# x of the first two batches loaded in halves, and one low part of the last adapter made earlier

## The reference

```python
w = L0_cond_weight[itok_B_1_14]                  # (8, 512, 512), gathered
y = jnp.einsum('bij,bkj->bik', x, w)             # x is (8, 128, 512)
q = y[:, 107:-1, :].mean(axis=1)
routing = jax.nn.softmax(q @ router_W.T + router_b, axis=-1)
base = y @ W.T + b
t = jnp.einsum('bsd,erd->bser', y, A)
lora = jnp.einsum('bser,eor,be->bso', t, B, routing) * 2.0
return x + base + lora
```

## Time and profile before

| | us |
|---|---|
| median of 3 runs | 72.85 |
| lowest, highest | 72.40, 73.01 |
| the profiled execution | 72.17 |
| span of its profile | 70.5 |
| PE busy | 65.9 (94%) |
| VectorE busy | 43.0 (61%) |
| ScalarE busy | 30.5 (43%) |
| loads and stores, 15.30 MB | 217 GB/s in the mean |

### The profile page before, as it was taken

The page is one execution under the profiler, slowest core; times in us unless marked ns, Lnnn a source line. Parts: engine busy times, 40 slices in busy tenths (PEclk is TensorE's granted clock), DMA queues, the critical chain, the costliest instruction groups (busy, mean ns, idle before and its releaser), DMA issues.

```text
span 70.5 us, 1142 instructions
## 1 busy us (share of the span) xinstructions
PE 65.9 (94%) x409; PEld 53.9 (76%) x409; DVE 43.0 (61%) x105; ACT 30.5 (43%) x62; POOL 1.2 (2%) x10
## 2 busy tenths in 40 slices
PE   2999989999999999999999999999999999999930
PEld 1332425743999988988988999888699999999920
DVE  1000022938999999779955999699554298250720
ACT  0800055487898993593036997300330330330000
POOL 5000000000000000000000000000000000000000
PEclk9999999999999999999999999999999999999999
DMA  0489999999999999999824014007230600600242
GB/s 0 112 265 384 358 387 409 417 405 414 409 407 412 407 409 405 409 409 402 333 64 104 9 42 107 0 0 298 47 88 19 151 3 9 284 14 0 69 154 74
DMA packets 7062, 15.30 MB, mean 217 GB/s; under 512 B 784, under 2 KB 3344, under 8 KB 7056
## 3 DMA queue, kind: packets, MB, share of 16 engines
q1 hardware_dynamic: 6624, 14.84, 56.2%
q10 hardware_dynamic: 432, 0.39, 2.1%
HBM read 12.08 MB, written 2.10 MB: 201 GB/s over the span
## 4 chain that ended last, share of the span: by engine, by line
PE 81%; DMA 8%; SPq 4%; issue 1%; DVE 1%
PE ps_o L556 32%; PE ps_t L556 8%; PE ps_o L573 8%; DMA wc_raw<-in_wcT_dram 8%; PE ps_y L516 5%; PE ps_y L539 4%; PE ps_y L538 4%; PE ps_y L540 4%; PE ps_yT L538 3%; PE ps_o L516 3%; PE ps_yT L540 3%; PE ps_yT L539 3%; PE ps_yT L549 3%; SPq L179 2%; SPq L184 1%
## 5 line engine op out<-in xcount | busy, mean ns | idle before, releaser
L556 PE MATMUL ps_o<-yT_hi,az_hi 128*128 128x256 f32 x64 | 18.1, 283 | 0.0
L556 PE MATMUL ps_o<-yT_lo,az_hi 128*128 128x256 f32 x64 | 17.8, 279 | 0.0
L556 PE MATMUL ps_o<-yT_hi,az_lo 128*128 128x256 f32 x64 | 17.8, 279 | 0.0
L556 PEld LDWEIGHTS ps_o<-yT_hi,az_hi 128*128 128x128 f32 x64 | 12.0, 188 | 0.1
L556 PEld LDWEIGHTS ps_o<-yT_hi,az_lo 128*128 128x128 f32 x64 | 12.0, 188 | 0.1
L556 PEld LDWEIGHTS ps_o<-yT_lo,az_hi 128*128 128x128 f32 x64 | 12.0, 188 | 0.0
L377 DVE TENSOR_TENSOR wc_lo<-wc_raw,wc_hi 128x1024 fp32r<-128x1024 f32 x10 | 11.9, 1211 | 0.1
L286 ACT CAST wc_hi<-wc_raw 128x1024 fp32r<-128x1024 f32 x10 | 10.0, 1052 | 0.0
L445 DVE SCALAR_TENSOR_TENSOR o_sb<-ps_o,rest_raw,xT_raw 128x256 f32<-128x256 f32 x16 | 7.1, 478 | 3.1 <-PE ps_o L573 3.1
L300 ACT ACTIVATE expd<-logit,nmax 128x8 f32<-128x8 f32 x8 | 2.3, 293 | 12.8 <-DVE nmax L427 12.8
L516 PE MATMUL ps_y<-wc_raw,xT_raw 128*128 128x512 f32 x16 | 7.4, 597 | 0.2 <-DMA wc_raw<-in_wcT_dram 0.2
(11 more groups left out here) (71 smaller groups left out, 111.9 us busy)
## 6 DMA issues: line engine op xcount, KB each, us to landing
wc_raw<-in_wcT_dram SPq DMA_DIRECT2D x16, 512.0 KB, 12.1
out_dram<-o_sb SPq DMA_DIRECT2D x3, 512.0 KB, 3.7
rest_raw<-in_rest_dram SPq DMA_DIRECT2D x2, 512.0 KB, 9.5
xT_raw<-in_xT_dram SPq DMA_DIRECT2D x2, 512.0 KB, 14.3
yT_raw<-y_turn SPq DMA_DIRECT2D x14, 64.0 KB, 2.1
xT_raw<-in_xT_dram SPq DMA_DIRECT2D x3, 256.0 KB, 6.7
out_dram<-o_sb SPq DMA_DIRECT2D x4, 128.0 KB, 1.9
rest_raw<-in_rest_dram SPq DMA_DIRECT2D x1, 278.0 KB, 7.6
```

The source lines that it names most:

```text
L556: last = mm(bank[:, 0:N2], stat[:, n, c, :], mov[pair][:, c].rearrange("p b s -> p (b s)"), start=(c == 0 and k == 0), stop=(stop and c == ...
```

## The change

Four things, in two places of the program.

- x of batches 0 and 1 comes in halves of two chunks (128 KB each), with a semaphore for each half. ScalarE issues the first half of x0 as its first instruction and no longer waits for the identity before it. SP issues the other three halves: the second of x0 after wc00, the first of x1 after wc01, the second of x1 after wc10.
- PE waits for a half of x where it used to wait for the whole; ScalarE's `hi_x1` waits for the second half of x1; VectorE waits for all four halves before the first `finish`.
- `lo_wc(7, (0,))`, the low part of the first half of the last adapter, moves from the start of g = 2 to g = 1, ahead of `lo_yT(5)`.
- On the host, x is laid out to match.

```diff
-def adapter_lora_kernel(nc, xT0, xT, ids, wcT, rest0, rest1, rest2, rest3, out):
+def adapter_lora_kernel(nc, xT0, xT1, xT, ids, wcT, rest0, rest1, rest2, rest3, out):
     _, _, _, C, S = xT.shape
-    ALONE = xT0.shape[0]
+    ALONE = 2 + xT1.shape[0]
     PAIRS = xT.shape[0] + ALONE // 2
...
         b_raw = rest_raw[:, FIRST + D:SECOND]
-        x_in = [sem(f"x{b}_in") for b in range(ALONE)] + [sem(f"x_pair{g}_in") for g in range(ALONE // 2, PAIRS)]
+        x_half_in = [[sem(f"x{b}_in{n}") for n in range(2)] for b in range(2)]
+        x_in = [None] * 2 + [sem(f"x{b}_in") for b in range(2, ALONE)] + [sem(f"x_pair{g}_in") for g in range(ALONE // 2, PAIRS)]
         wc_in = [[sem(f"wc{b}_in{n}") for n in range(2)] for b in range(B)]
...
                     .then_inc(wc_in[b][h], 16)
+            def load_x_half(b, h):
+                sp.dma_start(flat(xT_raw[:, b, half_of(h), :]), xT0[b, h]).then_inc(x_half_in[b][h], 16)
+
             def load_x(b):
-                sp.dma_start(flat(xT_raw[:, b]), xT0[b]).then_inc(x_arrived(b), 16)
+                sp.dma_start(flat(xT_raw[:, b]), xT1[b - 2]).then_inc(x_arrived(b), 16)
...
             load_wc(0, 0)
+            load_x_half(0, 1)
             load_wc(0, 1)
-            load_x(1)
+            load_x_half(1, 0)
             load_wc(1, 0)
+            load_x_half(1, 1)
             load_wc(1, 1)
...
             def hi_x1():
-                act.wait_ge(x_arrived(1), 16)
+                act.wait_ge(x_half_in[1][1], 16)
                 copy(flat(xT_hi[1][:, HALF:]), flat(xT_raw[:, 1, HALF:])).then_inc(x1_hi_ready, 1)
...
                                          scale=rout[:, i:i + 1]).then_inc(tsT_hi_ready, 1)
-            act.wait_ge(ident_ready, 1)
-            act.dma_start(flat(xT_raw[:, 0]), xT0[0]).then_inc(x_arrived(0), 16)
+            act.dma_start(flat(xT_raw[:, 0, half_of(0), :]), xT0[0, 0]).then_inc(x_half_in[0][0], 16)
             act.wait_ge(warm_ready, 1)
...
             lo_az(4)
             for b in range(2):
-                dve.wait_ge(x_arrived(b), 16)
+                for h in range(2):
+                    dve.wait_ge(x_half_in[b][h], 16)
             finish(0, 0)
...
                 router_parts(g)
                 if ahead:
-                    lo_wc(2 * g + 3, (0,))
+                    if g == 1:
+                        lo_wc(2 * g + 3, (0,))
                     turn(2 * g + 2)
...
                 for c in range(3):
                     finish(g, c)
+                if 2 * g + 5 == B - 1:
+                    lo_wc(2 * g + 5, (0,))
                 if ahead:
                     lo_yT(2 * g + 3)
-                if 2 * g + 4 < B:
+                if 2 * g + 5 == B - 1:
                     lo_x(2 * g + 5)
...
             def y_raw(b, c, bank):
-                if c == 0:
+                if b < 2 and c % HALF == 0:
+                    pe.wait_ge(x_half_in[b][c // HALF], 16)
+                elif c == 0:
                     pe.wait_ge(x_arrived(b), 16)
...
     wcT = contraction_first(wc).reshape(-1, P, 2, c // 2, d).transpose(0, 2, 1, 3, 4)
     arrays = {
-        "xT0": xT[:4].reshape(4, P, c * s),
+        "xT0": np.ascontiguousarray(xT[:2].reshape(2, P, 2, c // 2 * s).transpose(0, 2, 1, 3)),
+        "xT1": xT[2:4].reshape(2, P, c * s),
         "xT": np.ascontiguousarray(xT[4:].reshape(-1, 2, P, c, s).transpose(0, 2, 1, 3, 4)),
```

## The result

| | before | changed |
|---|---|---|
| median, us | 72.85 (7 runs, 72.35 to 73.94) | 73.18 (7 runs, 73.13 to 73.42) |
| ratio of the times, 95% interval | 1 | 1.0104 (1.0069 to 1.0139) |
| profiled execution, span | 72.17, 70.5 | 73.28, 71.5 |

In us, 1.0104 is +0.76 on 72.85.

The account below looks back on a forecast made before the run. The prediction took TensorE, busy 94% of the span, as the bound. Profiled 72.17 + 0.30 (opening) - 0.44 (late stage) = 72.03; on the scale of the 72.85 median that is 72.7 us, own range 72.3 to 73.1.

Parts of the forecast that it names:

- the issue is hidden by the backlog, and what counts is bytes: Opening, SP's queue: six microseconds of backlog hide two more issues; 0.13 MB more bytes make wc11 0.32 us later.
- wc01 may come 0.3 late, since PE waits for wc10 anyway: Opening, batch 0: wc01 some 0.3 later costs nothing net, as PE waits for wc10 until 10.02.
- +0.3 for the opening: Opening: wc11 0.32 us later makes PE's weight load 0.41 late, costing PE about 0.3 us.
- +4.3 us: Opening: three halves in SP's queue at 2.0 us fixed per load, nothing overlapping, 6.9 against 2.6 us; chance 0.01.
- the early issue gives nothing: Opening: ScalarE's earlier x0 issue gains nothing, at most 0.15 us, since PE's first real matmul waited for wc00.
- the late stage, -0.44: Batch 7: adapter 7's low part, moved into VectorE's idle time, removes PE's late weight loads, gaining 0.17 and 0.27 us.
- the long pieces: Batch 7 on PE: two matmuls taking 0.45 and 0.50 instead of 0.23 us, forecast to shrink to 0.23 to 0.3.
- The slack of yT_lo of batch 5 and of the router's parts: Late stage: both come about 0.4 us later on VectorE, within slack of 0.5 and 0.4 us before PE wants them.
- slower, through the small loads: Rival, opening: small loads each cost a 0.26 us pause, wc11 1.1 later, PE stands; +0.65, 73.5 us; chance 0.13.
- The forecast of the bytes alone: Opening: 0.13 MB more in SP's queue at 410 GB/s makes wc11 and every load behind it 0.32 us later.

Follow-up runs that it names:

- x0_half_after_wc01: The changed kernel without the late move and with x0's second half issued behind wc01 instead of ahead of it; ratio to the kernel before 0.9987.
- halves_only: The changed kernel without the late move of adapter 7's low part; ratio to the kernel before 1.0110.
- act_both: The changed kernel without the late move, with ScalarE sending both halves of x0 at once and SP only those of x1; ratio to the kernel before 1.0016.
- late_only: The kernel before with only the late move (low part of adapter 7's first half ahead of yT_lo of batch 5); ratio 0.9992.
- early_whole: The kernel before with only ScalarE's wait for the identity taken away, so x0 is sent whole at once; ratio 1.0019.
- the second look: The kernel before, unchanged, run and profiled once more; 71.67 us.
- spare_x_behind: act_both plus a 128 KB load of x by SP behind wc01, into a tile nobody reads; ratio to the kernel before 1.0029.
- spare_512k_between: act_both plus a 512 KB load by SP between wc00 and wc01, into a tile nobody reads; ratio to the kernel before 1.0204.
- spare_8k_between: act_both plus an 8 KB load by SP between wc00 and wc01, into a tile nobody reads; ratio to the kernel before 1.0108.
- wc01_issued_late: act_both with SP waiting for PE's sixth warm-up matmul between wc00 and wc01, no load between; ratio to the kernel before 1.0142.

## Why the prediction was wrong

- **Failed: the issue is hidden by the backlog, and what counts is bytes.** The prediction read the six microseconds from issue to use off wc11 and let them hide two more issues everywhere. For wc01 there is no such backlog: PE starts on wc00 2.9 us after wc01's issue. The half of x0 ahead of wc01 put its issue from 3.35 to 3.89 and its landing from 7.55 to 9.3, where the bytes account for 0.3; what makes the rest is open. By the runs, the half behind wc01 costs nothing (x0_half_after_wc01, 0.9987), ahead of it about 1.1% (halves_only, 1.0110).
- **Failed with it: wc01 may come 0.3 late, since PE waits for wc10 anyway.** PE stood 1.27 for wc01. Batch 0 took from 6.24 to 11.42, 5.18 instead of 3.67; the wait for wc10 was indeed gone. Up to the transposes that is 13.17 against 12.11, 1.06 later. The other 0.34 came between there and batch 2, where wc11 was 1.43 late.
- **Mis-sized: +0.3 for the opening.** +1.40 by the two profiles. Of wc11's 1.43 late, 0.32 is the bytes as computed and 0.6 the 0.25 MB that the queue did not move from 5.5 to 8.5; the rest isn't located. The profile of before had a good opening besides: act_both and late_only, without the slow stretch, reached batch 2 at 14.12 and 14.62.
- **The two rules of the Trainium skill.** Kernels act_both and halves_only differ only in who issues x0's second half, and with it in what stands ahead of wc01, and in the time, 1.0016 against 1.0110. By the Trainium skill, "DMA: Bandwidth & Descriptors", section "Issuing engines are not separate DMA queues", a second issuer saves only the sequencer's time, usually small beside the load. SP's issue takes 0.42 us here. The slot ahead of wc01 was worth 0.7 us by the times, whose intervals are too wide to tell that from 0.42, and 1.32 us in the two traces' batch 2 (14.12 and 15.44); so in the traces it is more than the sequencer's time. The prediction's +4.3 us rest on the Trainium skill's fit of 2.0 us fixed for each load, which stands in "DMA: Bandwidth & Descriptors", section "Anatomy of one DMA — SWDGE (gpsimd) path", and was measured on loads that GpSimd issues. SP and ScalarE issue these here, and no run shows a cost of that size.
- **Right: the early issue gives nothing.** PE started at 6.24 instead of 6.29, and early_whole gained nothing (1.0019).
- **Right in mechanism, lucky in size: the late stage, -0.44.** It is -0.40 in the two profiles, and the long pieces went as forecast. But the forecast was worked out from one execution of the kernel before, and the second look at it would have left 2.97 - 2.84 = 0.13 to gain. In the times the four pairs of kernels with and without the late move differ by 0.0006 to 0.0034 in their ratios, 0.04 to 0.25 us, all within their intervals: no gain is shown by any pair. The slack of yT_lo of batch 5 and of the router's parts held.
- **The rival "slower, through the small loads"** had the right sign and nearly the size, and only part of the mechanism: a small load does cost a pause, but in one place alone. x1's second half doesn't cost (act_both has it, 1.0016), and it isn't the number of loads. ScalarE's order did hold up the copy of y0, to 11.74 where batch 0 was done at 11.42, but the transposes came only at 13.17. The forecast of the bytes alone is not seen either: spare_x_behind is 1.0029 with an interval that holds both 0 and 0.3 us.

## What to carry to other kernels

Backlog is a property of a place in the queue, not of the queue: a load far down had six microseconds from issue to use, the second load had three. In the first microseconds of a kernel, issue the second load right behind the first, and put small loads that can wait behind it. Here the kernels whose wc01 was issued 2.8 us or more before PE could start on wc00 had a fast queue at 5.50:6.50, those with 2.2 to 2.5 us mostly a slow one; that is what these runs show, not a rule with a known cause. A change made of two edits has to be taken apart to see either: the halves hid whatever the late move gave. And before a term is taken from one profile, look at a second execution of the same kernel: the late stage's loss was 0.3 us smaller in it.

## What I had not expected of the hardware

wc01 issued at 3.87 to 4.2 was still issued over two microseconds before PE could start on the load ahead of it (6.2 to 6.5), and yet followed it slowly: 161 to 254 GB/s in 5.50:6.50 in six of the seven kernels that had it so (340 in the seventh; spare_512k_between, with 512 KB ahead of it, is not counted), where those with wc01 issued by 3.75 had 389 to 418.

The DMA share of that window doesn't tell a fast queue from a slow one: it is 1.04 at 406 GB/s in the kernel before and 1.04 at 242 GB/s in spare_8k_between. Where it is full and the bytes are few, packets take longer: in wc01_issued_late 56 packets filled 0.84 of the 16 engines' microsecond, some 0.24 us each, in the kernel before 115 filled 1.04, some 0.14 us each (an estimate, share times 16 us by the number of packets).
